# Attention and expert layer on one core: four scatters moved into the add turns, and products without a reader ahead of TensorE's waits in five slots

## The reference

```
x = x + xattn(layernorm(x), ctx)      # 16 heads of 16, softmax over 128 keys
x = x + ffn(layernorm(x))             # top 2 of 8 experts
# ffn: logits = n @ Wr + br; two largest, softmax over the two
#   h = n @ W1[e] + b1[e]; a, g = split(h); out_e = (silu(a) * g) @ W2[e] + b2[e]
#   out = sum over the two experts of gate * out_e
```

## Time and profile before

| | |
|---|---|
| median of 3 runs | 1207.9 us (1207.32 to 1212.38) |
| the profiled execution: own time | 1208.97 us |
| its span, first to last instruction | 1207.1 us |
| mean granted TensorE clock | 0.986 |
| PE busy | 1157.1 us, 96% of the span |
| DVE, ACT, POOL busy | 1002.0, 808.6, 628.5 us |

### The profile page before, as it was taken

One profiled execution on the slowest core, in us unless ns is written; L12 is line 12 of the kernel. 1 busy time (PEld: TensorE's weight loads), 2 busy tenths in 40 slices (PEclk: granted clock), 3 DMA queues, 4 the chain that ended last, 5 costly groups with the idle time before them and its releaser, 6 DMA issues. The chain is left out here.

```text
span 1207.1 us, 38337 instructions
## 1 busy us (share of the span) xinstructions
PE 1157.1 (96%) x12539; PEld 1037.3 (86%) x12540; DVE 1002.0 (83%) x2946; ACT 808.6 (67%) x1642; POOL 628.5 (52%) x736
## 2 busy tenths in 40 slices
PE   6999999999999999879989999999999999999996
PEld 5677777777777777559988999999999999999996
DVE  6789999999999999788877878888888888888883
ACT  5677777777777775568656666676676766766662
POOL 6346776677767765584733433443434434433433
PEclk9999999999999999889989999999999999999998
DMA  5122333333333334546767776666776766766753
GB/s 186 38 69 93 109 110 110 110 103 108 102 105 110 107 110 145 179 132 202 225 181 201 177 184 170 181 184 162 184 184 164 184 178 169 181 176 171 188 125 36
DMA packets 107679, 176.01 MB, mean 146 GB/s; under 512 B 14176, under 2 KB 82976, under 8 KB 107424
## 3 DMA queue, kind: packets, MB, share of 16 engines
q1 hardware_dynamic: 73472, 130.45, 34.2%
q0 software_dynamic: 26592, 36.46, 16.1%
q10 hardware_dynamic: 7488, 7.47, 1.8%
HBM read 126.21 MB, written 47.60 MB: 144 GB/s over the span
## 5 line engine op out<-in xcount | busy, mean ns | idle before, releaser
L1507 POOL DMA_INDIRECT out_rows<-y_gated,block_tokens x142 | 252.7, 1779 | 375.2 <-DMA out_rows<-y_gated,block_tokens 265.2
L583 PE MATMUL bank<-block_T_hi,w_hi 128*128 128x256 f32 x1136 | 327.7, 289 | 8.0 <-DVE block_T_lo L1222 8.0
L585 PE MATMUL bank<-block_T_hi,w_lo 128*128 128x256 f32 x1136 | 321.2, 283 | 0.0
L584 PE MATMUL bank<-block_T_lo,w_hi 128*128 128x256 f32 x1136 | 320.9, 282 | 0.0
L583 PEld LDWEIGHTS bank<-block_T_hi,w_hi 128*128 128x128 f32 x1136 | 217.8, 192 | 9.2 <-DVE block_T_lo L1222 9.2
L584 PEld LDWEIGHTS bank<-block_T_lo,w_hi 128*128 128x128 f32 x1136 | 217.6, 192 | 0.0
L585 PEld LDWEIGHTS bank<-block_T_hi,w_lo 128*128 128x128 f32 x1136 | 217.2, 191 | 0.0
L1232 DVE SCALAR_TENSOR_TENSOR act<-bank,block_b,silu_a 128x256 f32<-128x256 f32 x284 | 124.3, 479 | 78.2 <-ACT silu_a L818 45.1
L837 ACT ACTIVATE act_hi<-act 128x512 fp32r<-128x512 f32 x142 | 89.8, 633 | 143.0 <-DVE act L1232 141.5
L702 ACT ACTIVATE probs_T<-bank 128x512 f32<-128x512 f32 x256 | 132.2, 602 | 67.3 <-PE bank L439 67.3
L1205 DVE TENSOR_TENSOR w_lo<-w_raw,w_hi 128x1024 fp32r<-128x1024 f32 x142 | 167.2, 1219 | 4.7 <-ACT w_hi L803 4.3
(11 more groups left out here) (176 smaller groups left out, 2507.7 us busy)
## 6 DMA issues: line engine op xcount, KB each, us to landing
w_raw<-in_L_ffn_W SPq DMA_DIRECT2D x142, 512.0 KB, 5.7
block_rows<-routed_rows SPq DMA_DIRECT2D x71, 272.0 KB, 4.8
x_in<-in_x SPq DMA_DIRECT2D x64, 128.0 KB, 2.3
ctx_T<-in_ctx SPq DMA_DIRECT2D x16, 512.0 KB, 4.2
x_res<-in_x SPq DMA_DIRECT2D x64, 128.0 KB, 2.5
out_rows<-x SPq DMA_DIRECT2D x64, 128.0 KB, 2.4
w_lo<-in_L_ffn_W ACTq DMA_DIRECT2D x8, 512.0 KB, 4.4
out_rows<-y_gated,block_tokens POOLq DMA_INDIRECT x142, 6.1
```

Source lines behind the costliest of these rows:

```text
L583: mm(dst, w1h[k][:, c, at:at + P], xh[:, k, c, :], start=(c == 0), stop=False)
L584: mm(dst, w1h[k][:, c, at:at + P], xl[:, k, c, :], start=False, stop=False)
L585: last = mm(dst, w1l[k][:, c, at:at + P], xh[:, k, c, :], start=False, stop=(c == KC - 1))
L1507: nc.gpsimd.indirect_dma_start(out=out[:, :], out_offset=bass.IndirectOffsetOnAxis(ap=tk[:, u % U, t:t + 1], axis=0), in_=yg[:, u % 2, t, ...
```

## The change

In the first stage PE gets `keep_warm(n)`: n products of 128x128 by 128x256 from a weight tile that is in memory throughout, into bank 6, which nothing reads then. Eight stand ahead of `scores_T` and five ahead of `pv` in slots 60 to 64, and eight ahead of `squares_and_out(65)`: 5 x 13 + 8 = 73. On POOL the scatters of batches 60 to 63 leave slot 69 and stand singly behind the adds of blocks 3, 4, 5 and 6. No other engine's program changes, and no semaphore's final count.

```diff
+            def keep_warm(n):
+                for _ in range(n):
+                    mm(bank[6][:, 0:D], w_hi[3][:, 0, 0:P], w_hi[3][:, 0, :], start=True, stop=True)
...
                 ranks_and_logits(t)
+                if 60 <= t <= NB:
+                    keep_warm(8)
                 if real(t - 1):
                     scores_T(t - 1)
...
+                if 60 <= t <= NB:
+                    keep_warm(5)
                 if real(t - 1):
                     pv(t - 1, 0)
...
             for k in range(GB + 1):
+                if k == 0:
+                    keep_warm(8)
                 squares_and_out(NB + 1 + k)
...
-                if t == NB + GB + 1:
-
-                    pool.wait_ge(s_route, NB // GB)
-                    for b in range(NB - GB, NB):
-                        scatter(b)
...
-            turns(pool, expert_slot, GB - 1)
+            for b in range(NB - GB, NB):
+                k = GB - 1 + b - (NB - GB)
+                expert_slot(k // U, k % U)
+                pool.wait_ge(s_route, NB // GB)
+                scatter(b)
+            turns(pool, expert_slot, 2 * GB - 1)
```

## The result

The changed kernel takes 1199.04 us (median of 6 runs, 1197.41 to 1201.28) against 1207.61 for the kernel before (6 runs). The ratio is 0.9934, interval 0.9919 to 0.9949: 0.66% faster, 8.0 us by the ratio (8.6 by the two medians). Forecast were 7.7 us and 1200.2. The profiled span went from 1207.1 to 1197.5.

The account below looks back on a forecast made before the run. PE was taken as the bound in the expert slots, with DVE and ACT setting the pace in slots 8 to 10. Scatters 5.5 plus products 2.2 gave 7.7 us, median 1200.2; range 1196.5 to 1204.

Parts of the forecast that it names:

- place one: Ahead of block 7: PE idle 4.08 us, released by DVE's `x_lo`, late because `meta` waited 4.58 us for block 3's adds.
- margin of 2 to 3 us: Blocks 3 to 6: adds land 2 to 3 us before DVE's `meta` needs them, so moved scatters cost nothing.
- rivals 4 and 5: Adds land late behind scatters: by more than 0.6 us a turn, 1202.7 to 1204 (0.09), or over 10 us, 1227 (0.04).
- 0.6 us a turn: POOL's adds land in 7.1 us with a scatter behind each, 6.5 without; over four turns 2.4 us.
- terms of slots 6 and 7: DVE's chain: `x_lo` of block 7 4.0 us earlier, block 8's 5.3, or 5.7 followed operation by operation; 5.5 taken.
- what is won there stays won: Expert slots: all won ahead of the stretch from 700 to 800 us stays, since the engines then repeat the same slots.
- The products: Slots 60 to 63: if the 73 products keep the clock high, 3.3 us is saved; 2.2 taken, bounds 0 and 3.3.
- POOL's cap: Slot 61 can lose 1.1 us at most; POOL's low part of the context would be late in slot 62 by up to 0.8.
- Rival 3: PE alone counts at both places: 7.1 + 3.3 = 10.4 us, 1197.5; chance 0.12.
- Rival 2: Products bring nothing, as the clock falls anyway or POOL takes the gain: only 5.5 us, 1202.4; chance 0.2.
- rival 4: Single queue delays the adds: `meta` of blocks 8 and 9 waits 1 to 3 us, scatters bring 2 to 3.5; chance 0.09.

## Why the prediction was right, and where its terms were not

**The chain of place one** held in each link: scatters, late adds, `meta`, `x_lo`, idle PE. The adds of block 3 start at 588.90 (forecast 590.5), those of blocks 4 to 6 at 596.86, 607.72 and 616.98, 9.4 us apart on average (forecast 9.8), and no `meta` waits. The margin of 2 to 3 us was there: the adds of blocks 3 to 6 had landed by 596.86, 607.72, 616.98 and 627.03, and `meta` came at 600.22, 609.53, 619.15 and 629.81, which leaves 1.8 to 3.4 us. Even the whole list behind block 3's adds fits, if by 0.5 us, so rivals 4 and 5 are out. What they rest on, a landing that gets longer with scatters near, isn't seen: the eight adds of blocks 3 to 6 land in 6.6 us (median, 3.7 to 8.2) with a batch's scatter behind each, the next eight without one in 7.0 (5.8 to 7.8), and adds behind a list of eight or ten scatters took between 3.8 and 7.6 us in three kernels. They don't bear out that the prediction's 0.6 us a turn from the earlier trace rows was an effect of the scatters. The Trainium skill (DMA: Bandwidth & Descriptors, section SWDGE vs HWDGE vs iDMA) has only one queue allocated for GpSimd's transfers, and the prediction took from it that an add is late behind a scatter; these landings show no such cost.

**Its size**: forecast 5.5, measured alone 6.5 to 6.8. The terms of slots 6 and 7 came in at 4.2 and 1.5 (forecast 4.0 and 1.3 to 1.7). Missing was 1.1 us (0.8 in the changed kernel's profile) in slots 8 to 11, which the prediction held to be the same work in both kernels: it is, but the waits in it, DVE's for ACT, are not. That "what is won there stays won" holds only behind block 12 or so.

**The products** were forecast at 2.2 us, from 3.3 less POOL's cap. The profile has 2.8 at block 0 and 2.2 at block 6 and shows the cap, with the difference that PE waits for the rows of ACT and not for the low part of the context. But the two sides of that comparison are single executions. With scatters alone as the reference it is 1.2 to 1.7 us, within the noise; on the second chip it is not to be seen (block 0's `x_lo` at 562.00 with, 561.89 without), and alone, without the scatters moved, it is 0. The step that was wrong is the one that took the low clock of one execution for the clock of every execution: slot 60's half clock, 1.06 of the 3.3 us, was not there in the next trace of the same instructions.

**The sum** of 7.7 against 8.0 thus has two errors that cancel: 1.0 to 1.3 us too little for the scatters and 0.5 to 1.0 too much for the products. The range held; that the sum came within 0.3 us is in part luck. Rival 3 (PE alone counts, 10.4) is out by the ratio's interval, 6.2 to 9.8 us. Rival 2's 5.5 us is out too, narrowly, but its mechanism is not: with 6.5 to 6.8 us from the scatters, products that bring nothing would lie inside. A slip besides: 2 to 3.5 us and 2.2 give rival 4 a time of 1202.2 to 1203.7, not 1202.7 to 1204; nothing hangs on it.

What is still open: whether the products are worth anything; what the half clock behind the hole was worth by itself, since the hole was not on the chip where it was tried; why the lead of 2 us in the first stage dwindles over slots 8 to 12 when POOL is relieved; and what holds up PE and ACT on the second chip during the list of scatters.

## What to carry to other kernels

Before a gain ahead of a wait is counted, ask what ends that wait: a shorter first stage only lengthened it here (4.1 to 7.2 us) until the transfer chain behind it was shortened too. A long list of transfers on a queue that others depend on belongs behind the first thing that is due, and that order was worth nearly all; spreading it showed no gain in the time, only a wider margin. Where the clock flickers, take the price of it from more than one execution.

## What the runs showed that was not expected

The granted clock falls in different places in two executions of the same instructions with nearly the same waits: after 1.86 and 1.85 us of waiting in slot 60, `scores_T` took 1.92 us once and 1.06 the other time. The Trainium skill (TensorE: Matmul & The Clock Gate, Part 1) says of the slow products at a kernel's start that their number varies from run to run; these two traces show such a variation in the middle of a kernel. And during a list of ten indirect scatters PE and ACT can stand still without a wait for an instruction that the profile names: single products over 1 us apart and ACT idle for 6.3 us, so that `x_lo` comes 8 us late, in three profiles on one chip and in none on the other. That the list does it is inferred from the stretch, which is the same, and from its absence in all five profiles of that chip with the scatters spread; the way from one to the other was not measured.
